# Attention over an image on one core: theta and phi with their weights' remainders in one matmul, the correction copied and added back, a new order and eight banks for outputs

## What is computed

```python
theta = einsum('bhwc,cd->bhwd', x, W_theta)             # 1024 pixels x 32
phi   = maxpool2x2(einsum('bhwc,cd->bhwd', x, W_phi))   # 256 cells x 32
g     = maxpool2x2(einsum('bhwc,cd->bhwd', x, W_g))     # 256 cells x 128
beta  = softmax(einsum('bqd,bkd->bqk', theta, phi), axis=-1)
tmp   = einsum('bqk,bkv->bqv', beta, g)
return gamma * einsum('bhwv,vc->bhwc', tmp, W_o) + x
```

## Time and profile before

| | us |
|---|---|
| median of 3 runs (lowest, highest) | 241.42 (240.0, 241.47) |
| the profiled execution | 241.67 |
| its span in the trace | 239.8 |
| busy TensorE matmul, VectorE | 232.5, 205.8 |
| busy GpSimd, ScalarE | 167.1, 147.8 |

### The profile page before, as it was taken

One profiled execution on the slowest core, in us unless ns is written; L12 is line 12 of the kernel. 1 busy time (PEld: TensorE's weight loads), 2 busy tenths in 40 slices (PEclk: granted clock), 3 DMA queues, 4 the chain that ended last, 5 costly groups with the idle time before them and its releaser, 6 DMA issues.

```text
span 239.8 us, 4348 instructions
## 1 busy us (share of the span) xinstructions
PE 232.5 (97%) x1464; PEld 206.7 (86%) x1464; DVE 205.8 (86%) x475; ACT 147.8 (62%) x274; POOL 167.1 (70%) x119
## 2 busy tenths in 40 slices
PE   6999999999999999999999999999979999999994
PEld 4778888989989898998989889898968989889794
DVE  5699988989898898988889898898968989899775
ACT  3775957477494757748475684747648476545640
POOL 1487797868768686876868677696846968742870
PEclk9999999999999999999999999999999999999999
DMA  6792039195682928659293875919468193635854
GB/s 227 259 352 104 3 106 353 74 305 220 176 353 82 342 108 291 237 148 380 57 335 137 243 288 139 383 27 335 172 170 361 36 344 148 207 147 191 303 206 182
DMA packets 14934, 51.14 MB, mean 213 GB/s; under 512 B 1856, under 2 KB 2496, under 8 KB 14912
## 3 DMA queue, kind: packets, MB, share of 16 engines
q1 hardware_dynamic: 14512, 50.67, 60.0%
q10 hardware_dynamic: 400, 0.20, 0.3%
HBM read 33.95 MB, written 16.78 MB: 211 GB/s over the span
## 4 chain that ended last, share of the span: by engine, by line
PE 90%; DMA 3%; POOL 2%; DVE 2%; ACT 1%; issue 1%; SPq 0%; DVEq 0%; ACTq 0%
PE out L342 26%; PE proj L209 23%; PE proj L216 11%; PE shift L342 9%; PE score L253 6%; PE shift L306 6%; PE score L280 4%; POOL e_lo L556 2%; PE shift L209 2%; DMA theta<-neg_lo 2%; DMA x_t<-in_xt 1%; PE score L263 1%; PE shift L216 1%; PE proj L202 1%; PE out L280 1%
## 5 line engine op out<-in xcount | busy, mean ns | idle before, releaser
L556 POOL TENSOR_TENSOR e_lo<-e_sb,e_hi 128x512 fp32r<-128x512 f32 x64 | 81.9, 1294 | 48.0 <-ACT e_sb L480 48.0
L551 POOL TENSOR_TENSOR x_lo<-x_t,x_hi 128x1024 fp32r<-128x1024 f32 x30 | 71.8, 2399 | 8.9 <-ACT x_hi L436 8.9
L342 PE MATMUL out<-G_hi,e_hi 128*128 128x258 f32 x184 | 52.6, 286 | 0.0
L342 PE MATMUL out<-G_lo,e_hi 128*128 128x258 f32 x184 | 52.1, 283 | 0.0
L342 PE MATMUL out<-G_hi,e_lo 128*128 128x258 f32 x184 | 51.9, 282 | 0.0
L661 DVE SCALAR_TENSOR_TENSOR y_sb<-out,r_sum,x_n 128x256 f32<-128x256 f32 x92 | 44.5, 484 | 6.0
L209 PE MATMUL proj<-x_hi,w_hi 128*128 128x512 f32 x118 | 46.8, 396 | 0.0
L209 PE MATMUL proj<-x_hi,w_lo 128*128 128x512 f32 x118 | 46.6, 395 | 0.0
L635 DVE TENSOR_REDUCE neg_parts<-score 128x2 f32<-128x512 f32 x64 | 43.6, 686 | 1.1 <-PE score L253 0.2
L477 ACT ACTIVATE e_hi<-shift 128x512 fp32r<-128x512 f32 x60 | 36.0, 600 | 10.4 <-PE shift L306 9.6
L216 PE MATMUL proj<-x_lo,w_hi 128*128 128x512 f32 x118 | 37.3, 396 | 0.0
(11 more groups left out here) (99 smaller groups left out, 397.8 us busy)
## 6 DMA issues: line engine op xcount, KB each, us to landing
x_t<-in_xt SPq DMA_DIRECT2D x32, 512.0 KB, 5.3
x_n<-in_xn SPq DMA_DIRECT2D x32, 512.0 KB, 7.4
out<-y_sb SPq DMA_DIRECT2D x31, 512.0 KB, 6.2
w_sb<-in_w_proj SPq DMA_DIRECT2D x1, 256.0 KB, 2.7
theta<-neg_hi ACTq DMA_DIRECT2D x16, 4.0 KB
theta<-neg_lo SPq DMA_DIRECT2D x16, 4.0 KB
out<-y_sb SPq DMA_DIRECT2D x1, 256.0 KB, 2.0
wo_sb<-in_w_out SPq DMA_DIRECT2D x1, 128.5 KB, 5.5
```

Of the source, the lines that this page charges most:

```text
L342: last = nc.tensor.matmul(out_bank(i, t)[:, 0:GW], e[:, i % 2, KC * h + k, cells], G[:, i % 3, k, :], start=(n == 0), stop=(n == 3 * KC - 1))
L551: nc.gpsimd.tensor_tensor(x_lo[:, i % 2, h], x_t[:, i % 2, h], x_hi[:, i % 2, h].bitcast(f32), ALU.subtract).then_inc(x_lo_ready, 1)
L556: nc.gpsimd.tensor_tensor(e_lo[:, i % 2, n, :], e_sb[:, n, :], e_hi[:, i % 2, n, :].bitcast(f32), ALU.subtract).then_inc(e_lo_ready, 1)
```

## The change

**What it does.** The weights are packed anew in w_all: theta and phi once each (64 columns), their remainders beside them (64), then g high and g low. For one half of theta and phi:
- `pair_hi`: two matmuls with the high x give, in proj[h], the high product in rows 0 to 63 and the product with the weights' remainder (the correction) in rows 64 to 127.
- ScalarE's `copy_corr` copies the correction, rounded to float32r, to SBUF; `pair_lo` adds the two matmuls with the low x to rows 0 to 63; `add_corr` adds the correction by one matmul with a 64 x 64 unit matrix.
- theta now stands once in PSUM (rows 0 to 31). `theta_high` writes rows 0 to 31, `theta_low` rows 32 to 63, and the second high part, rows 64 to 95, is copied within SBUF by a transfer on SP's queue, `twin(i, h)`, 64 KB. `scores` of tiles 0 and 2 wait for it.
- From image 3 on the values go into out0 and out1 instead of proj, and phi_max into rows 64 to 95 of proj0. From image 1 to 12 the eight outputs go into six different banks (out0, proj1, shift0, out1, proj0, score1, out0, out1), and each waits for what lay there before.
- The order changes on all engines.

```diff
-PROJ = P + DV
+PAIR = 2 * DK
+PROJ = PAIR + DV
+VHI, VLO = 2 * PAIR, 2 * PAIR + DV
+PACKED = VLO + DV
...
-        w_hi, w_lo = sb("w_hi", [P, CC, PROJ], f32r), sb("w_lo", [P, CC, PROJ], f32r)
+        w_all = sb("w_all", [P, CC, PACKED], f32r)
+        eye = sb("eye", [PAIR, PAIR], f32r)
+        corr = sb("corr", [PAIR, 2, HALF], f32r)
...
+        def phi_max(i):
+            return outb[1][PAIR:THETA, 0:NK] if i < 3 else proj[0][PAIR:THETA, 0:NK]
+
         def value_bank(i, h):
-            return shift[h] if i < 2 else proj[h]
+            return shift[h] if i < 2 else proj[h] if i == 2 else outb[h]
...
         def out_bank(i, t):
+            if i == 0:
+                return (outb[0], outb[1], shift[0], shift[1], outb[0], outb[1], outb[0], outb[1])[t]
+            if i < LAST - 2:
+                return (outb[0], proj[1], shift[0], outb[1], proj[0], score[1], outb[0], outb[1])[t]
             if i == LAST - 2:
-                return (outb[0], outb[1], proj[0])[t % 3]
-            if i >= LAST - 1:
-                return proj[0] if i < LAST and t == 0 else (shift[1], outb[0], outb[1], shift[0])[t % 4]
-            return shift[t - 2] if t in (2, 3) else outb[t % 2]
+                return (outb[0], proj[1], proj[0])[t % 3]
+            return proj[0] if i < LAST and t == 0 else (shift[1], outb[0], outb[1], shift[0])[t % 4]
...
+            def twin(i, h):
+                pixels = slice(HALF * h, HALF * (h + 1))
+                sp.wait_ge(theta_hi_ready, 2 * i + h + 1)
+                sp.dma_start(theta[2 * DK:THETA, i % 3, pixels].bitcast(f32),
+                             theta[0:DK, i % 3, pixels].bitcast(f32)).then_inc(theta_twin[i % 3][h], 16)
...
@@ -157,10 +178,17 @@
             for h in range(2):
                 load_n(0, h)
             for h in range(2):
+                twin(0, h)
+            for h in range(2):
                 load_t(3, h)
+                if h == 0:
+                    twin(1, h)
             max_into_stack(0)
+            twin(1, 1)
             for s in range(2, LAST):
                 a, b, d = s, s - 1, s - 2
+                for h in range(2):
+                    twin(a, h)
                 max_into_stack(b)
...
+            def pair_hi(i, h):
+                if i == 0 and h == 0:
+                    pe.wait_ge(w_pair_lo_ready, 1)
...
-                elif i > 2:
+                elif i == 3:
...
+                elif i > 3:
+                    pe.wait_ge(y_ready, TILES * (i - 3) + (5 if h == 0 else 2))
+                if i > 0 or h > 0:
+                    pe.wait_ge(x_hi_ready, 2 * i + h)
+                for c in range(CC):
+                    if i == 0 and h == 0:
+                        pe.wait_ge(x0_hi_ready[c], 1)
+                    last = nc.tensor.matmul(proj[h][:, :], w_all[:, c, 0:P], x_hi[:, i % 2, h, c, :],
+                                            start=(c == 0), stop=(c == CC - 1), skip_group_check=True)
+                last.then_inc(corr_ready, 1)
...
+            def pair_lo(i, h):
+                if i > 0:
+                    pe.wait_ge(x_lo_ready, 2 * i + h + 1)
+                for n in range(CC):
...
+                    nc.tensor.matmul(proj[h][0:PAIR, :], w_all[:, c, 0:PAIR], x_lo[:, i % 2, h, c, :],
+                                     start=False, stop=False, skip_group_check=True)
...
+            def add_corr(i, h):
+                if i == 0 and h == 0:
+                    pe.wait_ge(eye_ready, 1)
+                pe.wait_ge(corr_copied, 2 * i + h + 1)
+                nc.tensor.matmul(proj[h][0:PAIR, :], eye[:, :], corr[:, h, :],
+                                 start=False, stop=True, skip_group_check=True).then_inc(tp_ready, 1)
...
+            def values_hi(i, h):
...
-                elif i > 1:
+                elif i == 2:
                     pe.wait_ge(theta_lo_ready, 2 * i + h + 1)
                     pe.wait_ge(phi_pooled, 2 * i + h + 1)
-                project(i, h, P, value_bank(i, h), g_ready)
+                elif i > 2:
+                    pe.wait_ge(y_ready, TILES * (i - 3) + 7 + h)
+                for c in range(CC):
+                    for w in (VHI, VLO):
+                        nc.tensor.matmul(value_bank(i, h)[:, :], w_all[:, c, w:w + DV], x_hi[:, i % 2, h, c, :],
+                                         start=(c == 0 and w == VHI), stop=False)
+
...
             def scores(i, n):
+                h = n // 2
+                if n in (0, 2):
+                    pe.wait_ge(theta_lo_ready, 2 * i + h + 1)
+                    pe.wait_ge(theta_twin[i % 3][h], twins(i))
                 if n == 0:
-                    pe.wait_ge(theta_lo_ready, 2 * i + 2)
...
+                elif t == 0:
+                    pe.wait_ge(g_pooled, 2 * later + 1)
+                elif t == 1:
+                    pe.wait_ge(theta_lo_ready, 2 * later + 2)
+                    pe.wait_ge(phi_pooled, 2 * later + 2)
                 elif i == LAST - 2:
-                    pe.wait_ge(y_ready, TILES * i + t - 3 + 1)
...
+                elif t == 2:
+                    pe.wait_ge(e_ready, 4 * i + 3)
+                elif t == 3:
+                    pe.wait_ge(g_pooled, 2 * later + 2)
+                elif t == 4:
+                    pe.wait_ge(phi_hi_ready, 2 * later + 2)
+                    pe.wait_ge(phi_lo_ready, later + 1)
+                elif t == 5:
+                    pe.wait_ge(neg_lo_ready, i + 2)
                 else:
-                    pe.wait_ge(y_ready, TILES * i + (t - 4 if t < 6 else t - 2) + 1)
+                    pe.wait_ge(y_ready, TILES * i + (1 if t == 6 else 4))
...
-            theta_phi(1, 0)
+            pair_hi(0, 0)
+            values_hi(0, 0)
+            pair_lo(0, 0)
+            add_corr(0, 0)
+            values_lo(0, 0)
+            pair_hi(0, 1)
+            values_hi(0, 1)
+            pair_lo(0, 1)
+            add_corr(0, 1)
+            values_lo(0, 1)
+
+            pair_hi(1, 0)
             scores(0, 0)
             scores(0, 1)
+            pair_lo(1, 0)
             values(1, 0)
+            add_corr(1, 0)
             scores(0, 2)
             scores(0, 3)
-            theta_phi(1, 1)
...
                 if s > 2:
-                    for h in range(2):
-                        theta_phi(a, h)
-                        scores(b, h)
-                        shifted(d, 2 + h)
-                    for h in range(2):
-                        values(a, h)
-                        scores(b, 2 + h)
+                    pair(a, 0)
+                    scores(b, 0)
+                    shifted(d, 2)
+                    add_corr(a, 0)
+                    pair(a, 1)
+                    scores(b, 1)
+                    shifted(d, 3)
+                    scores(b, 2)
+                    add_corr(a, 1)
+                    values(a, 0)
+                    scores(b, 3)
+                    values(a, 1)
                 if a < LAST:
-                    outputs(d, (0, 1, 2))
+                    outputs(d, (0, 1))
                     turn_max(b)
-                    outputs(d, (3, 4))
+                    outputs(d, (2, 3, 4))
                     mix(a)
                     output(d, 5)
...
-                nc.scalar.copy(theta[0:THETA, i % 3, HALF * h:HALF * (h + 1)],
-                               proj[h][0:THETA, :]).then_inc(theta_hi_ready, 1)
+                nc.scalar.copy(theta[0:DK, i % 3, HALF * h:HALF * (h + 1)],
+                               proj[h][0:DK, :]).then_inc(theta_hi_ready, 1)
+
+            def copy_corr(i, h):
+                act.wait_ge(corr_ready, 2 * i + h + 1)
+                nc.scalar.copy(corr[:, h, :], proj[h][PAIR:P, :]).then_inc(corr_copied, 1)
...
             first_x_high(0)
+            act.wait_ge(ident_ready, 1)
+            nc.scalar.copy(eye[:, :], ident[0:PAIR, 0:PAIR]).then_inc(eye_ready, 1)
+            copy_corr(0, 0)
             x_high(0, 1)
             theta_high(0, 0)
+            copy_corr(0, 1)
             x_high(1, 0)
             theta_high(0, 1)
+            phi_high(0)
+            copy_corr(1, 0)
             x_high(1, 1)
-            phi_high(0)
-            theta_high(1, 0)
...
                 if s > 2:
-                    for h in range(2):
-                        theta_high(a, h)
-                        exps(d, 2 + h)
+                    copy_corr(a, 0)
+                    theta_high(a, 0)
+                    copy_corr(a, 1)
+                    exps(d, 2)
+                    theta_high(a, 1)
+                    exps(d, 3)
                     phi_high(a)
...
+            g_high(LAST)
             exps(LAST - 1, 3)
-            g_high(LAST)
...
-                if a == 2:
+                if a < LAST:
                     g_low(a)
                     x_low(a + 1, 0)
-                    x_low(a + 1, 1)
-                elif a < LAST:
-                    x_low(a + 1, 0)
-                    g_low(a)
                     x_low(a + 1, 1)
...
             e_low(LAST - 1, 2)
+            g_low(LAST)
```

(23 more changed lines are left out.)

161 lines of the change are left out of this document (87 added, 74 removed).

## The result

The changed kernel takes **253.15 us** (median of 4 runs, 251.63 to 254.64); before, beside it, 241.12 (240.0 to 241.47). The ratio is 1.0485, 95% interval 1.0444 to 1.0526: slower by almost 5%. I had said 249.4, between 241.5 and 252.5. The direction was right; the time lies above the forecast and above the range. The profiled execution of after took 252.65 us, span 250.1, against a span of 239.8.

A forecast was written before the change was run, and what follows sets the result against it. TensorE, busy in 97% of the span, was taken as the bound, with VectorE the one to watch. Opening +7.1, stages +1.4, end -0.5 on 241.67 gave 249.7; less 0.25, 249.4 us, range 241.5 to 252.5.

The forecast's parts named there:

- Part 4: Opening: first scores wait for theta's twin transfer behind queued loads, TensorE idles 6.7 us; +7.1 us, bounds +2.8 to +9.
- +9: Opening's upper bound in us: matmuls behind the idle time run at the slow spacing, 0.2 us on some 10 matmuls.
- copies that come one behind another: Opening: ScalarE's copies of theta, correction and G hold VectorE up some 0.6 us (0 to 1.5).
- the transpose's place: Opening, block 2: the transpose waiting for VectorE stands one output earlier, leaving one more output of 0.73 us behind it.
- Parts 1 and 2: Repeating stage: 0.47 us of matmuls saved against a 0.58 us stall; 0.11 us longer a stage, +1.4 us over thirteen.
- part 2: Each stage's first output: TensorE waits for VectorE's g_pool(a,0) from 6.54 to 7.12 us, 0.58 us; bounds 0 to 0.8.
- one wait a stage at the first output: Sign expected in the profile after: a wait on g_max of 0.5 to 0.7 us, thirteen times.
- part 1: Each stage: one projection matmul per half goes, 0.233 us each; 0.47 us a stage, 6.1 us in all.
- Part 3: Each stage: ScalarE's correction copies, twin transfers, other new waits and GpSimd's reordering add nothing.
- Part 5: End: mix(LAST)'s 0.5 us wait for g_lo goes, as one e_lo stands ahead instead of two; -0.5 us, -1 to +0.5.
- more than I count: Rival, 253 us: slow spacing after the idle time (+9) and a 0.7 us stall, or correction copy 0.1 us late; 11%.

The follow-up runs named there:

- e6: The changed kernel with 26 matmuls on zeros put in TensorE's idle time ahead of scores(0,0); 250.78 us, ratio 1.0376.
- e1: The changed kernel with image 0's second high part of theta copied by ScalarE instead of a transfer on SP's queue; 246.53 us, ratio 1.0224.
- e10: e1 with six matmuls on zeros ahead of scores(0,0); 245.83 us, ratio 1.0196.
- e2: The changed kernel with the unit matmul over 128 rows, the added rows zero, instead of 64; 252.16 us, ratio 1.0464.
- e4: The changed kernel with the unit matmul over 128 rows and g_pool(a,0) ahead of maxima(b,2) on VectorE; 245.03 us, ratio 1.014.

## Why the prediction was right or wrong

**Part 4, the opening, is where the time was missed: +7.1 predicted, +10.06 measured.** The mechanism was right: the twin behind the loads, scores(0,0) waiting for it, released by that transfer (6.41 us against 6 to 7 predicted). Two sizes were off.
- The landing: near 18.5 predicted, 19.24 measured, +0.7.
- The step that failed is the clock. I had the slower matmul spacing in the rows and put it into the bound "+9"; in the sum I let the matmuls behind 6.7 us of idle time run at 0.233. They ran at 0.43, and scores(0,2) came 5.15 us behind the first instead of 2.58, +2.6. e6 shows the price by taking it away: 2.3 us are the clock, the other 0.2 to 0.3 stayed in e6 and have the size of the unit matmul's extra cost. The likeliest value should have carried it; the bound itself, two more, was of the right size, but with a late landing on top even +9 was passed.
- The rest was small: from VectorE's start on image 1 to its last maxima, 26.25 to 39.74 against 17.05 to 30.10, it lost 0.44 (predicted 0.6), and from there to stage 3 another 0.42 (0.73). Together 0.74 + 2.6 - 0.5 is the difference of 3.0 within 0.2.

The runs divide the 10.06 us: 5.74 went with the transfer (e1, 46.16 to 40.42), 2.05 more with the clock (e10), and 2.27 stay, for which the prediction had 0.6 for copies that come one behind another and 0.73 for the transpose's place; no run takes these apart.

**Parts 1 and 2, a stage: 14.26 predicted, 14.30 measured. That they agree is luck: the wait that I had priced is covered by a cost of nearly its size that I had not.**
- The step that failed: "All have 512 columns ... so I price narrower ones the same." The 98-row shift matmul was the row that I went by, and it was no guide for 64 rows. One unit matmul takes 0.57 us of TensorE and not 0.233, twice a stage: 0.67, more than the 0.47 that the removed matmuls give. TensorE arrived at 7.19 and not at 6.54. e2 shows the cause: the same matmul with 128 rows costs 0.23.
- The wait of part 2 exists, at the place and in the size forecast (6.54, stall 0.55 for 0.58 in e2), but in after it is covered. Of what I named as showing the steps right, "one wait a stage at the first output" did not appear. From the stage's length alone I would have taken part 2 as confirmed; only the list of waits tells that it isn't what binds.
- e4 shows that the 0.47 of part 1 is there once both are gone.

The Trainium skill ("TensorEngine Tiling (Array Packing)", Key Properties) says that a change of tiling mode, unlike a change of tile, drains TensorE. I missed this rule, which spoke against the change. The runs agree with it for 64 rows (0.34 us for going there and back) and show no such price for 64 columns: 128*64 stands between 128*128 ones at 0.23 a matmul. The other rule of the Trainium skill that I leaned on ("VectorE: DVE Perf Modes", "Two Vector instructions with no wait between them") held: the rows of after have 0.71 to 0.73 behind and ahead of an instruction on other partitions, and 0.61 otherwise.

**Part 3** held: no engine became late by the copies (ScalarE 10.14 us of 14.28). The weight load's "0.26 <-ACT corr" looks like a late copy, but ScalarE is not what it waits for: in e2 that gap is gone with the copies where they were. **Part 5** was wrong by 0.5: the 0.5 us wait for g_lo is gone from after's list of waits, but the last image's shifted scores wait 0.4 us for neg_lo there, and the end is level.

**The sum** on the profiled execution: opening +3.0, stages -1.1 (0.3 for 1.4; before lost 1.44 to one late transfer there, which I had counted in no stage), end +0.5, and what lies around the span 2.55 instead of 1.87, +0.7. That is 3.1, where 252.65 - 249.7 is 2.95. The rival "more than I count" (253) came nearest, with its first reason, the slow spacing; that its number fits too is luck, since the stall of 0.7 us a stage or the late copy that it also counted did not come. I gave it 11% and cut the range below it.

## What to carry to other kernels

Look at what stands in a queue ahead of the first transfer that something waits for: a 64 KB copy behind two 512 KB loads that nobody needed yet cost 6 us in this opening, and four issues in another order gave it back. Price a long idle stretch of TensorE with the slow matmuls behind it. Price a matmul of 64 rows between taller ones by its rows too, not by its columns alone. And where two limits lie within 0.1 us of each other, test both cures together: here each alone made the stage at most 0.03 us shorter, both together 0.61.
